# Row maxima of the second layer's context attention: spread by the matrix engine, or by two DMAs through DRAM

## What is computed

```python
q = query @ Wq.T + bq          # query: layer norm of x, 8 x 128 x 512
k = key @ Wk.T + bk            # key and value: the context, 8 x 2048 x 512
v = value @ Wv.T + bv
q, k, v = (t.reshape(B, -1, 16, 32).transpose(0, 2, 1, 3) for t in (q, k, v))
attn = softmax(q @ k.T / sqrt(32), axis=-1)
x = x + (attn @ v).transpose(0, 2, 1, 3).reshape(B, 128, 512) @ Wo.T + bo
```

## Time and profile before

| | us |
|---|---|
| median of 3 runs | 4111.04 |
| lowest and highest | 4108.64 and 4111.29 |
| the profiled execution | 4110.32 |
| its span, first to last instruction | 4108.5 |

### The profile page before, as it was taken

How to read it: one execution, slowest core, us unless ns; L and a number is a source line. 1 busy time by engine, 2 the same in 40 slices (tenths; PEclk the granted TensorE clock), 3 DMA queues, 4 the chain that set the end, 5 groups by cost and what they waited for, 6 DMA issues and landing times. The chain is left out here.

```text
span 4108.5 us, 73501 instructions
## 1 busy us (share of the span) xinstructions
PE 3995.8 (97%) x30656; PEld 2736.5 (67%) x30656; DVE 2177.3 (53%) x4381; ACT 1270.8 (31%) x3156; POOL 1003.8 (24%) x831
## 2 busy tenths in 40 slices
PE   8999999999999999899899999999999999998897
PEld 4777777777777778677465445666666666666675
DVE  5555555555555555255544324566665665546356
ACT  2222222222323222144233100333333333333344
POOL 2020202020202020022211000454454454445322
PEclk9999999999999999999999999999999999999899
DMA  4111111111111122211311400101101101101000
GB/s 144 62 62 62 62 62 62 62 62 62 62 61 63 58 66 73 88 29 35 108 42 48 163 0 29 55 24 45 58 24 45 58 25 45 50 1 45 11 2 21
DMA packets 127303, 219.86 MB, mean 54 GB/s; under 512 B 9088, under 2 KB 47616, under 8 KB 125184
## 3 DMA queue, kind: packets, MB, share of 16 engines
q1 hardware_dynamic: 118272, 181.60, 13.5%
q0 software_dynamic: 8704, 33.56, 2.5%
HBM read 198.35 MB, written 16.78 MB: 52 GB/s over the span
## 5 line engine op out<-in xcount | busy, mean ns | idle before, releaser
L577 PE MATMUL swishmax_attended<-swishmax_weights_t,swishmax_context 128*128 128x128 f32 x4096 | 520.1, 275 | 3.4 <-DVE swishmax_values_t L505 3.4
L1386 POOL TENSOR_TENSOR context_partial<-context_partial,context_weights_t 128x512 f32<-128x512 f32 x320 | 404.6, 1264 | 470.4 <-ACT context_weights_t L1397 452.7
L577 PEld LDWEIGHTS swishmax_attended<-swishmax_weights_t,swishmax_context 128*128 128x128 f32 x4096 | 487.9, 192 | 3.9 <-issue 3.9
L1546 PE MATMUL context_bank<-ahead_stream,ahead_staged 128*128 128x512 f32 x1024 | 473.3, 605 | 1.3 <-PEq L1072 1.3
L591 PE MATMUL swishmax_bank<-ahead_stream,ahead_w 128*128 128x512 f32 x1024 | 464.0, 596 | 7.2 <-DMA ahead_stream<-in_context_t_dram 7.2
L1445 DVE TENSOR_TENSOR context_weights_t<-context_score,context_shift 128x512 f32<-128x512 f32 x512 | 317.7, 683 | 231.9 <-PE context_score L1513 231.9
L435 ACT ACTIVATE swishmax_xes<-swishmax_score,swishmax_neg_max 128x512 f32<-128x512 f32 x256 | 177.2, 694 | 808.2 <-DVE swishmax_neg_max L470 808.2
L1426 DVE TENSOR_REDUCE context_neg_max<-context_score 128x1 f32<-128x512 f32 x512 | 317.9, 683 | 161.7 <-PE context_score L1498 161.4
L577 PE MATMUL swishmax_attended<-swishmax_weights_t,swishmax_sides 128*128 128x128 f32 x3072 | 384.9, 275 | 0.0
L1546 PEld LDWEIGHTS context_bank<-ahead_stream,ahead_staged 128*128 128x128 f32 x1024 | 184.0, 189 | 279.8 <-issue 272.2
L577 PEld LDWEIGHTS swishmax_attended<-swishmax_weights_t,swishmax_sides 128*128 128x128 f32 x3072 | 363.6, 192 | 0.0
(11 more groups left out here) (341 smaller groups left out, 5768.9 us busy)
## 6 DMA issues: line engine op xcount, KB each, us to landing
ahead_stream<-in_context_t_dram SPq DMA_DIRECT2D x78, 1024.0 KB, 5.8
swishmax_context<-in_context_dram POOLq DMA_DIRECT2D x32, 1024.0 KB, 5.9
swishmax_down<-_L_xattn_value_down_dram SPq DMA_DIRECT2D x64, 256.0 KB, 4.3
swishmax_up<-in_L_xattn_value_up_dram SPq DMA_DIRECT2D x32, 512.0 KB, 6.2
ahead_values<-ahead_staged SPq DMA_DIRECT2D x14, 1024.0 KB, 8.8
context_values<-ahead_values SPq DMA_DIRECT2D x56, 256.0 KB, 3.3
experts_w<-in_L_ffn_W_dram SPq DMA_DIRECT2D x16, 512.0 KB, 8.1
whole_x<-in_x_dram SPq DMA_DIRECT2D x8, 256.0 KB, 9.2
```

What stands on the lines that cost most here:

```text
L577: last = nc.tensor.matmul(product(i)[:, m, :], side(left, c, k, m), weights_t[:, n % 2, right, k, :], start=c == 0 and k == 0 and m == 0 a ...
L1386: link(nc.gpsimd.tensor_tensor(acc, acc, w_t[:, :, k, :], ALU.add))
L1546: last = nc.tensor.matmul(bank_t[:], w["k"][:, k, g * P:(g + 1) * P], context_t[:, c, k, :], start=k == 0, stop=k == DC - 1)
```

## The change

The maxima reach all partitions by another way. The steps `diagonal` and `spread` are gone, with the tile `diagonal`, the matmul and ScalarE's copy. In their place VectorE's step `minima` takes only the minimum. ScalarE then issues two DMAs a unit. `minima_out` writes the 128 x 4 minima to a DRAM tensor of 32 x 4 x 128, head by head, so that the 128 values of a head are contiguous there; each element is a run of 4 bytes. It is ScalarE's first item of the step at c = 0 after the unit. `minima_in`, ScalarE's last item of the same step, waits until the write has landed and loads the 2 KB row of the unit onto all 128 partitions of `shift`. The first `shift` of a unit waits for that load.

The second scores of a chunk, its shift and its exponentials run five steps after its first scores instead of four, and the weighted sum six instead of five. Sums and heads move from c = 1 to c = 2, the output of a batch from c = 2 to c = 3, the statistics for the later phase (`later`) from g = 1, c = 3 to g = 2, c = 0. There are ten key buffers instead of nine, and two semaphores for the value loads instead of four: a load waits for the one two places earlier.

```diff
-    KEYS, VALUES, SLOTS = 9, 12, 3
+    KEYS, VALUES, SLOTS = 10, 12, 3
...
-        diagonal = s.sb("diagonal", [P, HG, P])
+        minima_dram = nc.dram_tensor("context_minima", (NU, HG, P), F32, kind="Internal").ap()
...
-        value_landed = [s.sem(f"value_landed{n}") for n in range(4)]
+        value_landed = [s.sem(f"value_landed{n}") for n in range(2)]
...
-        LAG = NCH + 1
+        LAG = NCH + 2
...
-            out += [("sums", u - 2)] * (c == 1 and u >= 2) + [("spread", u - 1)] * (c == 0 and 1 <= u <= NU)
-            out += [("score_t", u - 1, c)] * (1 <= u <= NU) + [("value", u + 1, c)] * (u + 1 < NU)
+            out += [("sums", u - 2)] * (c == 2 and u >= 2)
+            out += [("score_t", *divmod(n - NCH - 1, NCH))] * (0 <= n - NCH - 1 < NU * NCH) + [("value", u + 1, c)] * (u + 1 < NU)
...
-            return out + [("output", b - 1)] * (g == 1 and c == 2 and b >= 1)
+            return out + [("output", b - 1)] * (g == 1 and c == 3 and b >= 1)
...
-            exps = [("exp", u - 1, c, r) for r in range(HG)] * (1 <= u <= NU)
-            out = [("key", u + 1, c)] * (u + 1 < NU) + [("spread", u - 1)] * (c == 0 and 1 <= u <= NU)
-            return out + exps[:2] + [("value", u + 1, c)] * (u + 1 < NU) + exps[2:]
+            exps = [("exp", *divmod(n - NCH - 1, NCH), r) for r in range(HG)] * (0 <= n - NCH - 1 < NU * NCH)
+            minima = [(what, u - 1) for what in ("minima_out", "minima_in")] * (c == 0 and 1 <= u <= NU)
+            out = [("key", u + 1, c)] * (u + 1 < NU)
+            return minima[:1] + out + exps[:2] + [("value", u + 1, c)] * (u + 1 < NU) + exps[2:] + minima[1:]
...
-                    if k >= 4:
-                        sp.wait_ge(value_landed[k % 4], 16 * (k // 4))
+                    if k >= 2:
+                        sp.wait_ge(value_landed[k % 2], 16 * (k // 2))
...
-                    elif what == "spread":
-                        act.wait_ge(full_a, ring.count(t))
-                        nc.scalar.copy(shift[:, u % 2], ring.bank(t)[:].rearrange("p (r q) -> p r q", q=P)).then_inc(out_a, 1)
+                    elif what == "minima_out":
+                        act.wait_ge(minima_set, u + 1)
+                        act.dma_start(minima_dram[u].rearrange("r q -> q r"), row_min[:], allow_slow_non_contiguous=True).then_inc(minima_landed, 16)
+                    elif what == "minima_in":
+                        act.wait_ge(minima_landed, 16 * (u + 1))
+                        act.dma_start(shift[:, u % 2].rearrange("p r q -> p (r q)"),
+                                      broadcast(minima_dram[u].rearrange("r q -> (r q)"))).then_inc(shift_landed, 16)
...
-                    elif what == "diagonal":
+                    elif what == "minima":
...
-                        link(nc.vector.tensor_reduce(row_min[:], neg_max[:, e], AX.X, ALU.min))
-                        if u:
-                            dve.wait_ge(full_a, ring.count(("spread", u - 1)))
-                        nc.vector.tensor_tensor(diagonal[:], ident[:].unsqueeze(1).broadcast_to([P, HG, P]),
-                                                row_min[:].unsqueeze(2).broadcast_to([P, HG, P]), ALU.mult).then_inc(diagonal_set, 1)
+                        nc.vector.tensor_reduce(row_min[:], neg_max[:, e], AX.X, ALU.min).then_inc(minima_set, 1)
...
-                            dve.wait_ge(out_a, ring.count(("spread", u)))
+                            dve.wait_ge(shift_landed, 16 * (u + 1))
...
-                    elif what == "spread":
-                        pe.wait_ge(diagonal_set, u + 1)
-                        last = nc.tensor.matmul(bank_t[:], ones[:], diagonal[:].rearrange("p r q -> p (r q)"), start=True, stop=True)
```

26 lines of the change are left out of this document (13 added, 13 removed).

## The result

| | before | after |
|---|---|---|
| median of 14 runs each, us | 4110.08 (4103.81 to 4112.7) | 4099.71 (4093.62 to 4103.55) |
| profiled execution, us | 4110.32 | 4102.55 |
| its span, us | 4108.5 | 4100.7 |

The ratio is 0.9975, with an interval of 0.9967 to 0.9983: the changed kernel is 10.4 us faster. The forecast was 4087.4 us with a range of 4079 to 4096 us. So the sign is as forecast, the size is less than half of the 23.6 us, and the time lies above the range.

The account below looks back on a forecast made before the run. TensorE was taken to bound the long stretch, busy 1203.94 of 1204.10 us. 25.5 + 2.1 - 4.0 = 23.6 us less than 4110.3 gives 4086.7, plus 0.7 for the median: 4087.4 us, range 4079 to 4096.

Parts of the forecast that it names:

- The spread: Long stretch, steps at c = 0: its removal saves TensorE 0.85 us for each of 30 units, 25.5 us.
- rival C: Steps freed of the spread: TensorE bound by something else, only part of 25 us shows; 4103 to 4115 us; chance 0.05.
- The two groups that leave the long stretch: One L1513 and one L1532 matmul group move behind the border into the tail: 2.1 us less.
- The issue by ScalarE: First in ScalarE's step: issuing the write, from 0.59 us up to 4 us, is hidden by a 4.35 us gap.
- The write: Row minima to DRAM, 512 runs of 4 bytes: lands in 2.5 us, bounds 1.7 and 8.8, costing the long stretch nothing.
- The broadcast: 256 KB onto 128 partitions before a unit's first shift: lands in 4.1 us, bounds 3.3 to 5.8, hidden.
- Rival A: First shift of each unit: broadcast lands late, each us beyond 6.6 costs 31 us; 4155 us at 8.8; chance 0.06.
- Two semaphores: Value loads, one due every second step some 18 us apart and taking 3.3 us: two instead of four cost nothing.
- The tail: Last stretch: chunk 125's exponentials end 3.3 to 5.0 us later, taken as 4 us; about 9 with a slow write.
- Rival B: Scattered write slow with its run count, ScalarE stands from about 9 us: 270 us, 4360 us, or some 4800; chance 0.03.

Follow-up runs that it names:

- the kernel with the held-back loads: Changed kernel with the later phase's weights loaded only after unit 31's broadcast has landed: 4097.58 us, ratio 0.9962.
- The early write: Changed kernel with minima taken behind the maxima of c = 3 and written in that step, wait and broadcast left in place: 4087.29 us, ratio 0.9952.

## Why the prediction was right in its sign and wrong in its size

1. *The spread.* Right. Steps at c = 0 take 8.80 us instead of 9.65, and rival C, that the room isn't used, didn't come.
2. *The two groups that leave the long stretch.* Right. With part 1 the forecast was 27.6 us for this stretch, and without the DMAs it is 28.4.
3. *The issue by ScalarE.* Right. It takes 0.38 us, and the key's bias behind it isn't late.
4. *The write.* This is the step that failed. I took 2.5 us between 1.7 and 8.8 us, and it is 9.5 us in the median and 14.4 us at worst. I had chosen the value by the lower row because it has the same 2 KB, and thought of its 128 runs of 16 bytes as a quarter of the work. They weren't comparable: not count or bytes set the landing, but that sixteen 4-byte pieces meet in 64 bytes. What the mistake cost lies in the sentence behind it, "either end costs the long stretch nothing". The upper row, 8.8 us, is equal to the time that ScalarE gives the write, 8.8 us after its issue. A bound that just touches the limit, from a transfer that isn't of the same kind, is no cover. By the forecast's own allowances (8.8 us for the write, and TensorE loses what the broadcast passes 6.6 us) write and broadcast together are harmless up to 15.4 us. The trace bears this limit out. When nothing is late, VectorE's first shift of a unit begins 15.0 us after the write's issue (in units whose steps take 8.80 us). In units 2, 6, 10, 14 and 18, all behind a 1 MB load, it began at 18.3, 15.9, 16.5, 15.4 and 16.2 us. TensorE's waits are what passes 15.4: 2.9, 0.5, 1.1, 0 and 0.8 us. Unit 2 lost 3.4 us more to the clock. In the kernel with the held-back loads units 2, 6, 10 and 18 began at 15.8, 16.3, 17.1 and 16.0 us and lost 0.4, 0.9, 1.7 and 0.6 us, with no fall of the clock. Unit 0 has shorter steps (6.5 us before it), so its limit comes sooner. There VectorE waited for the broadcast itself, and TensorE lost 0.8 us at step 6:

```profile
2585.19 2.48 DVE L1446 TENSOR_TENSOR context_weights_t<-context_score,context_shift 128x512 f32<-128x512 f32 x4 [3.07 <-DMA context_shift<-context_minima]
```

   The last 1.4 us of the 10.8 are at steps 21 and 49. There TensorE's scores take longer with VectorE not late, and I can't say why. The early write has two steps like them (0.9 and 0.7 us); without the DMAs, and with the pieces 64 or 512 bytes apart, there are none.
5. *The broadcast.* Right: 4.1 us taken, 4.1 us in the median. Its bound of 5.8 us is passed once, at unit 30 in the tail with 8.1 us. Rival A didn't come by itself. Where VectorE was late, it was because the broadcast was issued late.
6. *Two semaphores.* Right. In the kernels with one semaphore the long stretch is as short as without DMAs.
7. *The tail.* Its 4 us were worked out from the broadcast's landing. With the early write the tail grows by 4.4 us. But it also grows by 4.7 us without any DMA and by 4.2 us with the spread kept: there TensorE waits 5.9 and 4.1 us for GpSimd's sums, a limit that the working named and didn't price. That the number holds in both is luck. In the kernel without DMAs TensorE could begin unit 30's sums 41.4 us behind the border of step 124, and I had put GpSimd's part of them at 39.4 (3789.8 us on the clock of the earlier trace rows). The further 7.1 us are the two transfers. Unit 30's broadcast of 8.1 us puts unit 31's write 33.9 us behind the border instead of the 30.5 laid out, and that write lands after 9.6 us, so its broadcast is issued another 6.1 us later than I had it. Not all of these 9.5 us come out at the end. The likely reason is that the wait for GpSimd's sums now runs beside them; no run separates the two. With the loads held back, unit 31's write stood at 31.3 us and the tail was 2.2 us shorter. The mean granted clock of the tail fell as well, from 0.78 to 0.70; what that cost I can't separate.

Rival B was the right idea at the wrong price. It held the scattered write to be slow, let it cost only from about 9 us on, and had 270 us as its first price and a chance of 0.03. What lay between, a write of 9 to 14 us that stalls TensorE in a few units, had no case at all, and the range went only 4 us beyond the forecast's own.

On this the Trainium skill bears in "DMA: Bandwidth & Descriptors". Its section Rules for kernel authors speaks of one descriptor per element and a 19-fold difference; measured by the least landings, the write is 7.9 / 1.4 = 5.6 times as slow as the 16-byte runs, and 512 single elements 64 bytes apart cost only 1.8 / 1.4 = 1.3 times. So the trace agrees with the direction of the rule but not with the count of elements as its cause. Its section Anatomy of one DMA, which describes DMAs issued by GpSimd, says that a semaphore can't be raised before the last byte is confirmed to be in its memory. This write is issued by ScalarE, and its trace agrees: in the changed kernel the packets of a write lie within 0.4 to 1.6 us, the last of them is over 5.3 us after the issue at the latest and 1.3 us in most units, and the semaphore is raised 7.9 us after the issue at best.

## What to carry to other kernels

Before a small result is sent through DRAM, look at which bytes of DRAM the pieces of different partitions share, and give each partition one contiguous run, or 64 bytes of its own; then count from the issue to the landing, with the load that is issued just ahead of it, and not from the bytes. When a cost is bounded from both sides, compare the upper bound with the limit in the plan: if the two are within a microsecond of each other, the bound says nothing, and the case beyond it needs a chance and a price of its own. The cheapest remedy here was to issue the transfer earlier, as soon as its data exist, and to leave the wait where it is.

## What the runs showed of the hardware that I had not expected

- Pieces of 4 bytes from many partitions that lie side by side in DRAM land 7.9 us after the issue at best; the same pieces 64 or 512 bytes apart land in 1.8 us, and 128 pieces of 16 bytes side by side in 1.4 us.
- A small write issued 0.6 us behind a 1 MB load on another engine's queue lands 3 to 5 us later than the quickest one without it, and its first packet starts 3.6 to 4.0 us after the issue instead of 0.9.
- An addition of 128 x 512 elements, one operand in PSUM and one in SBUF, takes 1095 ns instead of 682 when the SBUF operand is read at a step of 16 bytes.
- In one execution a shift that came 3.3 us late held TensorE for 2.9 us, and about 2 us after it went on its granted clock fell to 0.50 for more than 6 us, which cost another 3.4 us. In the kernel with the held-back loads waits of up to 1.7 us had no fall of the clock behind them. A group that waits between its matmuls shows as busy, so such waits are read from a group's duration and not from the idle time.
